# Attention scores of the first two image pairs as fp32 products, and the results in two stores

## The reference, cut to what matters

```
layer 0:  q = Wq x + bq, k = Wk x + bk (8 channels each);  v = Wv x + bv (32 channels)
          attn = softmax(q^T k, over keys);   x = gamma * (Wo (v attn^T) + bo) + x
layer 1:  the same with its own q, k and a v of 64 channels, no Wo:   x = x + v attn^T
layer 2:  batch norm, relu, 3x3 convolution with weights mean(|w|) * sign(w), twice; plus x
layer 3:  a 4x4 covariance per quarter channel over all positions, its Cholesky factor,
          a triangular solve, a small mixing matrix and a bias
```

## Time and profile before

| | before |
|---|---|
| median of 3 runs | 65.8 us |
| profiled execution, its time | 65.95 us |
| its span | 64.2 us |
| granted TensorE clock, mean | 0.989 |
| PE, DVE, ACT, POOL busy | 55.8, 47.0, 41.8, 21.5 us |

### The profile page before, as it was taken

One profiled execution on the slowest core, in us unless ns is written; L12 is line 12 of the kernel. 1 busy time (PEld: TensorE's weight loads), 2 busy tenths in 40 slices (PEclk: granted clock), 3 DMA queues, 4 the chain that ended last, 5 costly groups with the idle time before them and its releaser, 6 DMA issues.

```text
span 64.2 us, 2136 instructions
## 1 busy us (share of the span) xinstructions
PE 55.8 (87%) x803; PEld 34.7 (54%) x803; DVE 47.0 (73%) x124; ACT 41.8 (65%) x135; POOL 21.5 (34%) x64
## 2 busy tenths in 40 slices
PE   5997999499997995995999897999899999999900
PEld 2345454275653623441655564689776997955500
DVE  0069998698958888498895888899479978577630
ACT  0713289999997797979979196690039563278830
POOL 5000683830645508258212107317303050025000
PEclk9999999999999999999999999999999999999995
DMA  0888881000000000000000000000000000000054
GB/s 0 216 232 199 282 303 51 0 0 10 0 0 0 0 5 0 10 0 5 0 5 0 0 0 0 10 0 10 0 0 0 10 0 10 0 0 0 0 167 160
DMA packets 2457, 2.71 MB, mean 42 GB/s; under 512 B 400, under 2 KB 2064, under 8 KB 2448
## 3 DMA queue, kind: packets, MB, share of 16 engines
q1 hardware_dynamic: 2016, 2.26, 11.8%
q10 hardware_dynamic: 432, 0.33, 1.5%
HBM read 2.06 MB, written 0.52 MB: 40 GB/s over the span
## 4 chain that ended last, share of the span: by engine, by line
PE 63%; DVE 19%; issue 7%; POOL 3%; ACT 2%; DVEq 0%; POOLq 0%; ACTq 0%
PE bank L942 12%; PE bank L717 12%; PE both L834 10%; PE bank L757 4%; DVE negmax L1083 3%; DVE cut L1095 3%; PE both L728 3%; PE bank L800 2%; DVE x L1135 2%; PE bank L775 2%; DVE qk L1112 2%; PE bank L792 2%; PE both L918 2%; PE bank L978 2%; PE bank L742 2%
## 5 line engine op out<-in xcount | busy, mean ns | idle before, releaser
L562 ACT ACTIVATE probs<-bank 128x512 f32<-128x512 f32 x16 | 8.6, 586 | 1.4 <-PE bank L800 1.3
L717 PE MATMUL bank<-const-bfloat16-1.0 128*64 128x512 bf16 x60 | 8.7, 433 | 0.8 <-PEq L1390 0.8
L542 ACT ACTIVATE bank<-bank,negmax 128x256 f32<-128x256 f32 x20 | 9.0, 453 | 0.6 <-DVE negmax L1083 0.4
L834 PE MATMUL both<-probs,vt 128*64 128x256 f32 x56 | 7.7, 390 | 0.0
L1083 DVE TENSOR_REDUCE negmax<-bank 128x2 f32<-128x512 f32 x10 | 6.7, 686 | 1.0 <-PE bank L775 0.6
L542 ACT ACTIVATE both<-both,negmax 128x256 f32<-128x256 f32 x12 | 5.4, 447 | 1.6 <-DVE negmax L1083 1.6
L369 POOL TENSOR_TENSOR cut<-cut 64x256 f32<-64x256 f32 x7 | 4.3, 611 | 6.2 <-DVE cut L1095 5.4
L942 PE MATMUL bank<-hi,taps 64*64 64x225 f16 (+2 forms) x126 | 5.9, 267 | 0.1
L942 PE MATMUL bank<-lo,taps 64*64 64x225 f16 (+2 forms) x126 | 5.9, 265 | 0.0
L385 POOL TENSOR_TENSOR shift<-negmax,lntot 128x4 f32<-128x4 f32 x8 | 1.6, 202 | 12.2 <-issue 11.8
L717 PEld LDWEIGHTS bank<-const-bfloat16-1.0 128*64 128x64 bf16 x60 | 3.5, 120 | 3.5 <-issue 1.6
(11 more groups left out here) (163 smaller groups left out, 121.9 us busy)
## 6 DMA issues: line engine op xcount, KB each, us to landing
cw<-conv_w SPq DMA_DIRECT2D x2, 288.0 KB, 4.8
x<-x_in SPq DMA_DIRECT2D x4, 128.0 KB, 3.0
kst<-consts SPq DMA_DIRECT2D x1, 428.0 KB, 5.9
out<-res SPq DMA_DIRECT2D x3, 128.0 KB, 1.9
aw<-attn_w ACTq DMA_DIRECT2D x1, 128.0 KB, 2.5
aw<-attn_w SPq DMA_DIRECT2D x1, 128.0 KB, 3.6
out<-res ACTq DMA_DIRECT2D x1, 128.0 KB, 1.8
half<-select SPq DMA_DIRECT2D x1, 96.0 KB, 3.1
```

The source lines that it names most:

```text
L542: nc.scalar.activation(part, part, ACT.Exp, bias=negmax[:, i % 2, n:n + 1], accum_out=total[:, i % 2, n:n + 1]).then_inc(total_out, 1)
L562: nc.scalar.activation(probs[:, i % 2, g], pb_t[g][:].rearrange("p (t n) -> p t n", t=CH), ACT.Exp).then_inc(exp_out, 1)
L717: mm(bank[lanes(h)], filler[:, lanes(h)], filled, start=True, stop=True)
L834: last = mm(mixed(i)[g * C:(g + 1) * C], vt[:, i % 2, t, g * C:(g + 1) * C], probs[:, i % 2, g, t, :], start=(t == 0 and i < ITERS - 1), s ...
```

## The change

Pairs 0 and 1 (the list `DIRECT`) no longer go through bf16 parts. Their projection writes four blocks of 32 rows with four matmuls, the queries to one PSUM bank and the keys to another, placed so that each image's 8 rows start at row 0 or 32 of SBUF after the copy. VectorE copies the queries with their bias (`direct_queries`), ScalarE the keys (`direct_keys`), both as fp32 to `fp_qk`. `direct_scores` multiplies them as fp32 with a contraction over 8 rows; for pair 0 both images are interleaved, for pair 1 the second image comes after the first. `scores_t` of pairs 0 and 1 does the same with queries and keys exchanged. The GpSimd steps of pair 1, the two subtractions of pair 0 on VectorE and the two `replicate` steps go, as do two of the three `keep_warm` calls. The lists of steps of TensorE, VectorE, ScalarE and GpSimd are written in another order at the start. The transfer of x for pair 2 is issued before that of the selector matrix. At the end SyncE issues two stores of two pieces each instead of three stores, and ScalarE none.

```diff
-WARM_START = (6, 3, 4)
+WARM_START = 6
...
+        fp_qk = sb("fp_qk", [C, len(DIRECT), 2, N])
...
-            return {1: banks[7], 3: pb_v}.get(i, pb_pv)[:, N:2 * N]
+            return (pb_v if i == 3 else pb_pv)[:, N:2 * N]
+
+        def direct_banks(i):
+
+            return {0: (pb_pv[:, N:2 * N], pb_s[1][:, 0:N]), 1: (banks[7][:, N:2 * N], pb_s[2][:, 0:N])}[i]
+
+        def splits(i):
+
+            return sum(n not in DIRECT for n in range(i))
...
+            sp.dma_start(xs[0][:, quarter(2)], x[:, quarter(2)]).then_inc(x_in[2], 16)
             sp.dma_start(half[:], select).then_inc(half_in, 16)
-            for b in range(2, PAIRS):
-                sp.dma_start(xs[0][:, quarter(b)], x[:, quarter(b)]).then_inc(x_in[b], 16)
+            sp.dma_start(xs[0][:, quarter(3)], x[:, quarter(3)]).then_inc(x_in[3], 16)
...
-            for n in range(len(PIECES) - 1):
-
-                sp.wait_ge(res_act, n + 1)
-                sp.wait_ge(res_dve, n + 1)
-                sp.dma_start(out[:, quarter(n)], res[:, quarter(n)]).then_inc(stored, 16)
-            sp.wait_ge(stored, 16 * len(PIECES))
+            for n in range(2):
+
+                sp.wait_ge(res_act, 2 * n + 2)
+                sp.wait_ge(res_dve, 2 * n + 2)
+                both_pieces = slice(2 * n * N, 2 * n * N + 2 * N)
+                sp.dma_start(out[:, both_pieces], res[:, both_pieces]).then_inc(stored, 16)
+            sp.wait_ge(stored, 32)
...
-            pool.wait_ge(part2_out, 1)
-            parts1(1)
-            parts2(1)
-            pool.wait_ge(part2_out, 2)
...
+            def direct_keys(i):
+
+                act.wait_ge(proj_mm, i + 1)
+                nc.scalar.activation(fp_qk[:, DIRECT.index(i), 1], direct_banks(i)[1][lanes(1)], ACT.Identity,
+                                     bias=prm[lanes(1), P_DIRECT:P_DIRECT + 1]).then_inc(keys_out, 1)
...
             first_bias()
+            direct_keys(0)
+            direct_keys(1)
+            totals(0, 0)
             value_weights()
             value_bias()
-            act.wait_ge(rep_mm, 1)
-            nc.scalar.activation(qk[:, 0, 1], pb_s[2][:, 0:N], ACT.Identity).then_inc(k0_out, 1)
-            totals(0, 0)
             totals(0, 1)
             logs(0)
-            first_values()
             totals(1, 0)
             totals(1, 1)
             logs(1)
+            first_values()
...
-            act.wait_ge(res_act, len(PIECES))
-            act.wait_ge(res_dve, len(PIECES))
-            act.dma_start(out[:, quarter(3)], res[:, quarter(3)]).then_inc(stored, 16)
...
+                if i in DIRECT:
+                    for r in range(P // BLOCK):
+                        first = w + r * CQ
+                        to = slice(r * BLOCK, (r + 1) * BLOCK)
+                        last = mm(direct_banks(i)[r // G][to], aw[:, first:first + BLOCK], x_of(i), start=True, stop=True)
+                else:
+                    for h in range(2):
+                        last = mm(proj(i)[lanes(h)], aw[:, w + h * C:w + (h + 1) * C], x_of(i), start=True, stop=True)
...
+            def direct_scores(i, images):
+
+                pe.wait_ge(part0_out, i + 1)
+                pe.wait_ge(keys_out, DIRECT.index(i) + 1)
+                for g in images:
+                    if 2 * i + g >= 3:
+                        pe.wait_ge(total_out, CH * (2 * i + g - 2))
+                q, k = (fp_qk[:, DIRECT.index(i), o] for o in range(2))
+                for t in range(CH):
+                    for g in images:
+                        rows = slice(BLOCK * g, BLOCK * g + CQ)
+                        last = mm(pb_s[(2 * i + g) % 3][:, t * N:(t + 1) * N], q[rows, t * P:(t + 1) * P], k[rows],
+                                  start=True, stop=True)
+                        if t == CH - 1:
+                            last.then_inc(s_mm, 1)
...
+                            q, k = (fp_qk[BLOCK * g:BLOCK * g + CQ, DIRECT.index(i), o] for o in range(2))
+                            mm(pb_t[g][:, t * N:(t + 1) * N], k[:, t * P:(t + 1) * P], q, start=(t == 0), stop=False,
+                               skip_group_check=True)
+                            continue
...
-            keep_warm(WARM_START[0], pb_t[0])
+            keep_warm(WARM_START, pb_t[0])
 
             project(0)
+            project(1)
+            direct_scores(0, range(G))
+            project(2)
             value_weights()
-            project(1)
-            replicate(0)
-            project(2)
-            scores(0)
+            direct_scores(1, (0,))
+            direct_scores(1, (1,))
             scores_t(0)
             project(3)
-            replicate(1)
+            replicate(2)
             values(0)
-            pe.wait_ge(part0_out, 3)
-            keep_warm(WARM_START[1], pb_pv)
-            scores(1)
-            replicate(2)
-            keep_warm(WARM_START[2], pb_pv)
             shifts_to_rows(0)
...
-            def later_parts(i):
-
-                dve.wait_ge(part0_out, i + 1)
-                some = cut[PART_ROWS[1]:P, i]
-                ve.tensor_tensor(some, some, tops(some), ALU.subtract).then_inc(part1_out, 1)
-                dve.wait_ge(part1_out, i + 1)
-                some = cut[PART_ROWS[2]:P, i]
-                ve.tensor_tensor(some, some, tops(some), ALU.subtract).then_inc(part2_out, 1)
+            def direct_queries(i):
+
+                dve.wait_ge(proj_mm, i + 1)
+                ve.tensor_scalar(fp_qk[:, DIRECT.index(i), 0], direct_banks(i)[0][lanes(0)],
+                                 prm[lanes(0), P_DIRECT:P_DIRECT + 1], None, ALU.add).then_inc(part0_out, 1)
...
-            first_parts(0)
-            later_parts(0)
-            first_parts(1)
-            queries_keys(0)
+            direct_queries(0)
+            direct_queries(1)
+            maxima(0, 0)
             first_parts(2)
-            maxima(0, 0)
             maxima(0, 1)
-            queries_keys(1)
-            first_parts(3)
             maxima(1, 0)
             maxima(1, 1)
+            first_parts(3)
             queries_keys(2)
...
+    for r in range(P // BLOCK):
+        params[r * BLOCK:r * BLOCK + CQ, P_DIRECT] = a["L0_conv_bk" if r // G else "L0_conv_bq"]
```

More of the change, by code:

```diff
@@ L40 @@
 PART_ROWS = (0, 64, 96)
+DIRECT = (0, 1)
 TAPS = 9
@@ L58 @@
 P_W3 = 11
-P_COLS = P_W3 + Q * Q
+P_DIRECT = P_W3 + Q * Q
+P_COLS = P_DIRECT + 1
 K_ID = 0
@@ L366, in parts1 @@
                 pool.wait_ge(part0_out, i + 1)
-                pool.wait_ge(part1_out, i)
+                if splits(i):
+                    pool.wait_ge(part1_out, splits(i))
                 some = cut[PART_ROWS[1]:P, i]
@@ L371, in parts2 @@
             def parts2(i):
-                pool.wait_ge(part1_out, i + 1)
-                pool.wait_ge(part2_out, i)
+                pool.wait_ge(part1_out, splits(i) + 1)
+                if splits(i):
+                    pool.wait_ge(part2_out, splits(i))
                 some = cut[PART_ROWS[2]:P, i]
@@ L395, in _ @@
             pool.wait_ge(ones16_set, 1)
[L397 to L400 removed]
             parts1(2)
             parts2(2)
[L403 removed]
+            pool.wait_ge(part2_out, 1)
             shifts(0)
@@ L407, in _ @@
             parts2(3)
-            pool.wait_ge(part2_out, 4)
+            pool.wait_ge(part2_out, 2)
             shifts(1)
@@ L414, in _ @@
             parts2(4)
-            pool.wait_ge(part2_out, 5)
+            pool.wait_ge(part2_out, 3)
             shifts(3)
@@ L419, in _ @@
             parts2(5)
-            pool.wait_ge(part2_out, 6)
+            pool.wait_ge(part2_out, 4)
             shifts(4)
@@ L424, in _ @@
             parts2(6)
-            pool.wait_ge(part2_out, 7)
+            pool.wait_ge(part2_out, 5)
             shifts(5)
@@ L429, in _ @@
             parts2(7)
-            pool.wait_ge(part2_out, 8)
+            pool.wait_ge(part2_out, 6)
             pool.wait_ge(prm_in, 16)
@@ L726, in project @@
                 w = A_P0 if i < PAIRS else A_P1
-                for h in range(2):
-                    last = mm(proj(i)[lanes(h)], aw[:, w + h * C:w + (h + 1) * C], x_of(i), start=True, stop=True)
+                if i in DIRECT:
[6 more added lines that the diff above has]
+                        last = mm(proj(i)[lanes(h)], aw[:, w + h * C:w + (h + 1) * C], x_of(i), start=True, stop=True)
                 last.then_inc(proj_mm, 1)
             def replicate(i):
-                pe.wait_ge(part2_out, i + 1)
-                if i == 0:
+                pe.wait_ge(part2_out, splits(i) + 1)
+                if splits(i):
+                    pe.wait_ge(qk_out, splits(i))
+                else:
                     pe.wait_ge(half_in, 16)
-                else:
-                    pe.wait_ge(qk_out, i)
-                    pe.wait_ge(k0_out, 1)
                 for o in range(2):
                     for h in range(2):
-                        to = pb_s[2][lanes(h), 0:N] if i == 0 and o == 1 else pb_rep[lanes(h), o * N:(o + 1) * N]
```

(4 more changed lines are left out.)

15 lines of the change are left out of this document (5 added, 10 removed).

## The result

The changed kernel took 73.93, 74.37, 75.16 and 76.97 us (median 74.8); the kernel before took 65.73 to 66.2 beside it (median 65.9). The ratio is 1.1245, interval [1.1148, 1.1341]. The forecast was 67.0 with a range to 68.2: the sign was right, and the time lies 6.6 us above the range. The profiled execution is the slowest, 76.97 us.

The account below looks back on a forecast made before the run. The prediction took the kernel to be bound at the start by a chain of waits through all engines. It summed 65.95 + 1.3 (later scores(4)) - 0.1 (stores) = 67.15 profiled, 67.0 as median; range 65.3 to 68.2.

Parts of the forecast that it names:

- the sign: Whole kernel: the change makes it slower, 67.0 us forecast after 65.95 for the profiled execution before.
- 0.65 for a projection: TensorE, projections: four records, two by two, take 0.65 us, read from the profile before.
- slow at the first product: Rival, chance 0.06: waiting before 4.92 us leaves TensorE slow; projection and first product cost 0.4 + 0.7 more, 68.1 us.
- price of a direct fp32 group: TensorE, direct scores: four fp32 matmuls of 256 columns hold it 0.9 us, where the bf16 group held it 0.22.
- pairing of images: TensorE, interleaved direct groups: the two images' records run in pairs, so a group's eight records take 0.9 us.
- half price: Rival, chance 0.18: direct products cost 0.5 us a group, or delay is taken up later; 65.8 us, no change.
- unpaired groups: Rival within a shared chance of 0.12: a group's two images do not pair, three groups grow by 0.9 each, 69.7 us.
- bf16 price: Rival, chance 0.11: a contraction over 8 rows costs 0.22 us a group; scores(2) 0.8 earlier, 64.9 us.
- The four column blocks of a projection: TensorE, direct projections: all four blocks assumed to run beside each other, project(1) taking 5.0 to 5.5 us.
- `values(0)` late: TensorE at the start: result of values(0) at 11.75 us, where it was out at 9.04.
- VectorE's queue held behind `first_parts(3)`: VectorE at the start: idle some 1.4 us there waiting for values(0), so scores(2) starts at 13.2 us, 0.85 later.
- the stores: End of the kernel: two larger stores gain 0.1 us, bounds 0.15 gained to 0.2 lost.

Follow-up runs that it names:

- e13: The changed kernel run once more, unchanged, on the same chip as e12: 74.22, 71.11, 72.34, 72.23 us.
- e1: The changed kernel with two pairs of constant products over 128 rows between project(0) and project(1), where TensorE paused: ratio 1.0553 to the kernel before.
- e8: e1 plus seven pairs of constant products over all rows after values(0): 69.77, 70.07, 69.8, 71.6 us.
- e5: The changed kernel with direct products over 64 rows per image instead of 8, image 1's rows holding a constant: 67.59, 67.34, 69.0, 67.6 us.
- e9: e5 with queries and keys of the direct pairs copied as bf16 instead of fp32: ratio 0.9836 to the kernel before.
- e4: The kernel before with only the end changed, two stores of two pieces from SyncE: median 65.96 us, ratio 0.9998.
- e16: e3 run again unchanged: 71.45, 67.22, 67.67, 69.46, 75.26, 67.75 us.
- e7: The kernel before with scores(0), scores(1), scores_t(0) and seven pairs of constant products over 8 rows: 70.73, 70.89, 67.25, 65.86 us.
- e3: The changed kernel with direct products over 32 rows instead of 8, all holding data: 69.6, 72.01, 69.6, 67.27 us.
- e12: The changed kernel with the additions of e10 and e1 together: ratio 1.0404 to the kernel before.
- e10: The changed kernel with constant bf16 products in rows 64 to 127 beside the direct ones, except scores_t(1): 74.96, 77.02, 67.39, 67.51 us.

## Why the prediction was wrong

**The step that failed** is TensorE's rate. Every price of the forecast (0.9 us for a group, 0.65 for a projection) is one of the upper level, applied from 5.0 us on, and nothing in the sum asked whether the changed work would still bring and keep that level. The runs showed in its place records of 0.63 us instead of 0.38 up to 30 us (changed) or from 8.8 to 25.3 us (e13). Beside the earlier trace rows the forecast even noted that `project(0)` took 1.12 at a granted clock of 1.00, and passed over it. The rival "slow at the first product" had half of the mechanism, the waiting before x of pair 1, and the wrong extent: it let the lower level end after 0.4 + 0.7 us of extra cost, where it lasts to 30 us. The other half, that the narrow products let the level fall after it has come (e1, e8, e13), no rival had. That the forecast had the sign right is no merit of the mechanism: most of what was measured is not in its sum. Of the excess over the kernel before, 8.9 us by the medians, 1.7 are the schedule (e5: 67.6) and 7.2 the level.

**What was right**, by e5:

- The price of a direct fp32 group and the pairing of images. In e5 the records take 0.38, and the group starts at 5.67 and lets the next projection begin at 6.74: 0.9 and a change of kind, with the pass of 0.17 hidden. The half price and the unpaired groups are refuted, for 8 rows too (0.37, in pairs, in e1); the bf16 price is what e9 shows for bf16 operands alone.
- The four column blocks of a projection run beside each other: their first records start at 3.46 and 3.47 in the changed kernel, and eight records take 0.64 in e5, as four did before. As the Trainium skill (TensorE: Matmul & The Clock Gate, Part 3) says, such blocks run concurrently; the trace agrees, with those starts.
- `values(0)` late, and VectorE's queue held behind `first_parts(3)`: idle 1.50 where some 1.4 was forecast.

**Sizes that were off:**

- `scores(2)` came 0.37 later than forecast in e5 (13.57). VectorE started `first_parts(3)` 0.26 late (12.06, 11.8 forecast), of which 0.11 is x of pair 1 (5.11 instead of 5.0) and the rest `values(0)`; its own part took 0.11 more (1.51, 1.4 forecast).
- This was carried on: `exps(1)` started at 17.95 (17.5 forecast) and `scores(4)` at 21.90 (21.4). The profiled execution lost 1.6 us (67.59 after 65.95) instead of the 1.2 of the sum, 0.1 of it for the stores, which gave nothing (e4).

**What stays open:** why one execution of the same kernel keeps the level and the next doesn't (67.22 to 75.26 in e16), of which the length of the pause is at best a part; why the level comes at 3.5 us in e5 and not before 5.4 in others with the same instructions up to there; and whether a number of rows between 32 and 64 would do. That the rows at work decide rests on counts of executions, not on a reading of the chip, and how 7.2 us divide between the pause and the narrow products was not measured. No version here beats the kernel before and does its whole job.

## What to carry to other kernels

Before a price from the profile is moved to new work, ask at which of TensorE's two levels it was measured, and whether the new work will be run at that level: compare durations of one shape along the timeline, for the granted clock may read 1.00 over records at the lower level. A product over 8 or 32 rows costs the same time as one over 64, but in these runs it counted for less in keeping TensorE's level: in the first microseconds of a kernel, where everything stands in one chain, give it wide neighbours and leave no pause before it, or don't use it. And the maxima's earlier start was worth nothing, because fp32 products moved the values behind the scores, where VectorE's queue waits for them.

## What the runs showed of the hardware that was not expected

- TensorE busy for all of 8.00 to 10.20 us (e1) fell to the lower level; busy for 10.6 us in e7 (3.4 to 14.0), it did not leave it. Keeping it busy is not enough.
- The granted clock reads 0.50 to 0.52 once the level has been up and falls (e1, e3, e13), and 1.00 at the lower level of a program's start, even when that lasts to 30 us (changed kernel).
- bf16 products in rows 64 to 127 run beside fp32 products in rows 0 to 39 at no cost in either's duration when the level is up (e12: 0.38 and 0.37). At the lower level they held the next projection up by 1.6 us (e10).
- Four stores of 128 KB and two of 256 KB are the same to 0.2%.
